# The second expert layer sorted by expert, with three of its four chunks routed inside the attention stage before it

## The chip, the cores and the metric

One core of a Trainium2 chip runs the whole program. The metric is device time in microseconds. TensorE (PE) multiplies, VectorE (DVE), ScalarE (ACT) and GpSimd (POOL) work on what it leaves, and SyncE (SP) issues most transfers. Each engine has its own queue and works it off in order; the queues meet at semaphores.

## The reference, cut to what matters

Input is 2048 tokens of 128 numbers. Six layers follow each other, each on the layer norm of the running sum `x`:

```python
x = x + 0.5 * expert_ffn(ln(x))      # first expert layer
x = x + attention_0(ln(x))           # 16 heads of 8, causal, then wo and bo
x = x + 0.5 * expert_ffn(ln(x))      # second expert layer: the one that is changed
x = x + 0.5 * ternary_ffn(ln(x))
x = x + attention_1(ln(x))
x = x + 0.5 * ternary_ffn(ln(x))

def expert_ffn(x):
    expert = argmax(softmax(x @ Wr.T))               # one of 8 per token
    inter = gelu(x @ W1[expert] + b1[expert])        # 128 -> 512, for each token its own expert
    y = inter @ Wo + bo + x
    return layer_norm(y) * gamma + beta
```

## The kernel before, in words

Tokens are cut into 16 blocks of 128 and 4 chunks of 512 (`NB`, `NCH`, `CH`, `BPC` = 4 blocks per chunk). Each layer is a function that writes one piece of program for every engine. `order` is the order in which a layer takes the chunks; a layer may make some of the next layer's norms (`Norms.make`, `given` says how many are there when the layer begins).

*Expert layer* (`expert_layer`, L282). For each chunk TensorE transposes the normed rows (L399) and makes the router's logits (L408). VectorE chooses an expert per token (`choose`, L651 to L667) as a one-hot row. Then all 8 experts are run over all 512 tokens: TensorE spreads an expert's 0/1 mask over the partitions (L428), ScalarE copies it (L587), VectorE masks both halves of the split input (L839), and TensorE adds three 512-column matmuls for each of the 4 tiles of the hidden layer (L443). A token of another expert gives zeros, so the sum over experts is the right expert's. Biases (L453), gelu (L578), down projection (`down`, L467), and `finish` on VectorE (L676 to L686): sum, norm, gamma, add to `x_res`. The input is split into a high and a low float16 part so that float16 matmuls keep the accuracy.

*Attention stage* (`attention_layer`). Work is written out in turns. A turn has one "quad" (128 keys against up to 512 queries of one group of four heads): scores (L1237 and L1186 are its matmuls with the running maxima), exps on ScalarE (L1319), values (L1215). Beside it stand some "units": scores of a later step whose row maxima VectorE takes (`part_max`, L1356). A step is a group of heads and a chunk of queries; `STEPS` lists them, and `units_beside_quads` deals the units out over the turns so that each step's maxima are there in time. When a step has ended, its output is scaled (L1385, L1389); after a chunk's last step come "turned" and "project", with the sum into `x_res` (L1360 to L1365). Three PSUM banks are used in rotation for all of this (the ring), and TensorE waits for VectorE to have read a bank.

*Ternary layer* (`ternary_layer`). Transposes (L890), ScalarE's high part (L933), VectorE's low part (L964), up matmuls (L914), relu (L942), down (L899), sum into `x_res` (L982). Norms that are not given are made between the low parts.

## Time and profile before

| | us |
|---|---|
| median of 3 runs | 1215.2 (1214.64 to 1215.71) |
| the profiled execution | 1215.68 |
| its span | 1213.9 |
| TensorE busy | 1091.9 (90%) |
| VectorE busy | 1006.6 (83%) |
| ScalarE busy | 664.6 (55%) |
| GpSimd busy | 65.8 (5%) |
| mean granted TensorE clock | 0.975 |

The span is from the first to the last instruction; 1.8 us of the execution lie around it. Busy time is a sum over stages with different limits, so the table is read stage by stage. The granted clock is 1.0 at 2.4 GHz and 0.5 at 1.2 GHz.

### The profile page before, as it was taken

Reading aid. Unit: us, or ns where it says so; the run is one execution under the profiler, and the core shown is the slowest. Engines: PE = TensorE matmul, PEld = TensorE weight load, DVE = VectorE, ACT = ScalarE, POOL = GpSimd, SP = SyncE. Lnnn points to the kernel's source line nnn. Section 1 sums busy time; section 2 is a strip of 40 time slices with the busy share of each in tenths; the row PEclk is TensorE's granted clock in tenths of the full one; section 3 lists DMA queues with packets and bytes.
Section 4 is the critical chain, followed back from the end, with each engine's and each line's share of the span. In section 5 each row is a group of like instructions: output and inputs, shape, how many; then the busy total and the mean of one; then the engine's idle time right before and its main releaser. Section 6 shows DMA issues by size and latency. Waiting matters only on the chain.

```text
span 1213.9 us, 34232 instructions
## 1 busy us (share of the span) xinstructions
PE 1091.9 (90%) x14757; PEld 492.3 (41%) x14757; DVE 1006.6 (83%) x2343; ACT 664.6 (55%) x861; POOL 65.8 (5%) x62
## 2 busy tenths in 40 slices
PE   1898976999999999999699987689999999999988
PEld 1455552333333333334345555433333333333436
DVE  8977568999999999886547657799999999998764
ACT  0322222556777777777332214145667777887773
POOL 5111001000000000000100100100000000000000
PEclk9999988999999999999799998899999999999999
DMA  5100034100000000000000000620000000000001
GB/s 158 36 1 1 1 98 117 33 3 2 2 3 2 3 2 3 3 2 3 1 1 2 1 1 1 181 64 3 2 3 2 2 2 2 3 2 3 4 3 35
DMA packets 23555, 24.07 MB, mean 20 GB/s; under 512 B 3134, under 2 KB 21220, under 8 KB 23404
## 3 DMA queue, kind: packets, MB, share of 16 engines
q1 hardware_dynamic: 22252, 18.73, 5.4%
q0 software_dynamic: 1152, 3.15, 1.0%
q8 instruction: 116, 1.90, 0.7%
q14 instruction: 35, 0.29, 0.1%
HBM read 13.20 MB, written 8.39 MB: 18 GB/s over the span
## 4 chain that ended last, share of the span: by engine, by line
PE 55%; DVE 37%; issue 4%; ACT 3%; DMA 1%; SPq 0%; DVEq 0%; ACTq 0%
DVE part_max L1356 25%; PE psum L1215 12%; PE psum L1237 11%; PE psum L443 10%; PE psum L1186 6%; PE psum L467 3%; ACT hidden L1319 2%; PE psum L1201 2%; PE psum L899 2%; PE psum L1243 1%; DVE xn L168 1%; PE psum L1264 1%; DVE norm_v L151 1%; PE psum L914 1%; PE psum L428 1%
## 5 line engine op out<-in xcount | busy, mean ns | idle before, releaser
L1356 DVE TENSOR_REDUCE part_max<-psum 128x1 f32<-128x512 f32 (+3 forms) x1120 | 677.1, 668 | 52.7 <-PE psum L1243 35.3
L1319 ACT ACTIVATE hidden<-psum 128x1024 f32<-128x1024 f32 (+3 forms) x640 | 539.0, 895 | 220.8 <-PE psum L1186 219.7
L1237 PE MATMUL psum<-k_slots,q_slots 128*32 128x512 f16 (+3 forms) x5120 | 389.9, 355 | 31.4 <-DVE part_max L1356 13.5
L1215 PE MATMUL psum<-hidden,v_aug 128*9 128x512 f32 (+3 forms) x2560 | 290.3, 530 | 0.1
L1237 PEld LDWEIGHTS psum<-k_slots,q_slots 128*32 128x32 f16 x5120 | 123.3, 95 | 286.2 <-DVE part_max L1356 193.1
L443 PE MATMUL psum<-parts,w_parts 128*128 128x512 f16 x768 | 179.5, 385 | 1.9 <-DVE parts L839 1.9
L1186 PE MATMUL psum<-q_slots,k_slots 32*128 32x512 f16 (+3 forms) x1472 | 141.3, 328 | 9.6 <-ACT hidden L1319 7.7
L443 PEld LDWEIGHTS psum<-parts,w_parts 128*128 128x128 f16 x768 | 73.6, 99 | 82.4 <-issue 5.7
L587 ACT CAST parts<-psum 128x512 f16<-128x512 f32 x64 | 37.2, 588 | 107.1 <-PE psum L428 107.1
L1243 PE MATMUL psum<-ident_bf,later_keys 128*32 128x128 bf16 (+2 forms) x1408 | 91.5, 250 | 0.0
L1186 PEld LDWEIGHTS psum<-q_slots,k_slots 32*128 32x128 f16 x1472 | 42.0, 91 | 99.7 <-ACT hidden L1319 49.0
L1201 PE MATMUL psum<-later_keys,ident_bf 128*32 128x128 bf16 x2048 | 74.8, 223 | 4.4 <-ACT hidden L1319 1.9
L1215 PEld LDWEIGHTS psum<-hidden,v_aug 128*9 128x9 f32 x2560 | 61.6, 90 | 34.9 <-ACT hidden L1319 1.6
L839 DVE TENSOR_TENSOR parts<-parts 128x1024 f16<-128x1024 f16 x64 | 46.8, 755 | 18.3 <-ACT parts L587 18.2
L1201 PEld LDWEIGHTS psum<-later_keys,ident_bf 128*32 128x32 bf16 x2048 | 39.7, 95 | 50.5 <-issue 19.4
L1243 PEld LDWEIGHTS psum<-ident_bf,later_keys 128*32 128x32 bf16 x1408 | 38.4, 99 | 18.6 <-issue 17.5
L625 POOL TENSOR_TENSOR x_plus<-xn,bo_bc 128x512 f32<-128x512 f32 x8 | 13.8, 1722 | 517.2 <-DVE xn L168 478.5
L245 ACT COPY xn_t<-psum 128x512 f32<-128x512 f32 x8 | 4.7, 588 | 57.0 <-PE psum L220 57.0
L467 PE MATMUL psum<-wo_sb,hidden 128*128 128x128 f32 x256 | 31.7, 285 | 3.7 <-ACT hidden L578 3.7
L954 POOL TENSOR_TENSOR x_plus<-x_res,fb_half 128x512 f32<-128x512 f32 x8 | 10.0, 1265 | 447.0 <-DVE xn L168 447.0
L467 PEld LDWEIGHTS psum<-wo_sb,hidden 128*128 128x128 f32 x256 | 31.3, 201 | 5.6 <-ACT hidden L578 4.7
L676 DVE TENSOR_TENSOR x_plus<-psum,x_plus 128x512 f32<-128x512 f32 x8 | 5.5, 691 | 33.8 <-PE psum L467 33.8
(168 smaller groups left out, 731.4 us busy)
## 6 DMA issues: line engine op xcount, KB each, us to landing
q_slots<-q_rows SPq DMA_DIRECT2D x8, 512.0 KB, 3.8
k_slots<-k_rows POOLq DMA_DIRECT2D x24, 128.0 KB, 4.2
q_rows<-parts SPq DMA_DIRECT2D x18, 128.0 KB, 3.0
k_rows<-parts SPq DMA_DIRECT2D x18, 128.0 KB, 2.8
q_slots<-in_L_ffn_W_dram SPq DMA_DIRECT2D x2, 1024.0 KB, 6.5
k_slots<-k_rows SPq DMA_DIRECT2D x8, 128.0 KB, 4.0
q_slots<-nm_parts SPq DMA_DIRECT2D x64, 4.0 KB
out_dram<-x_res SPq DMA_DIRECT2D x4, 256.0 KB, 2.3
```

Source lines behind the costliest of these rows:

```text
L443: last = pe.matmul(psum[:, t, :], w1_parts[:, e, wp, t * P:(t + 1) * P], x_mask[:, k % NX, xp, :], start=(e == 0 and (wp, xp) == (0, 0)), ...
L467: last = pe.matmul(psum[:, DOWN_BANK, i * D:(i + 1) * D], hidden[:, n % 2, t, i * P:(i + 1) * P], wo2_sb[:, t, :], start=(t == 0), stop=(t ...
L587: act.copy(mask_sb[:, k % NX, :], psum[:, MASK_BANKS + k % 2, :]).then_inc(mask_ready, 1)
L839: dve.tensor_tensor(x_mask[:, k % NX, :, :], x_parts[:, n % 2, :, :], mask_sb[:, k % NX, :].rearrange("p (a t) -> p a t", a=1).broadcast_t ...
L899: last = pe.matmul(psum[:, 6 + n % 2, i * D:(i + 1) * D], hidden[:, n % 2, t, i * P:(i + 1) * P], tw2_t[:, t, :], start=(t == 0), stop=(t ...
L1186: last = pe.matmul(psum[:, S_BANKS + 2 * (tile % 2) + par, cols], k_slots[rows, G * g + 2 * pr + par, j * P:(j + 1) * P], q_slots[rows, g, ...
L1201: last = pe.matmul(psum[rows32(m), S_BANKS + 2 * (tile % 2) + par, off:off + P], ident_bf[:, rows32(m)], later_keys[:, :], start=(pr == 0) ...
L1215: last = pe.matmul(psum[VW * h:VW * h + DH + 1, O_BANK, off:CH], v_aug[:, j, G * g + h, :], probs[:, (2 * n + h // 2) % NP, h % 2, off:CH] ...
L1237: last = pe.matmul(psum[rows32(m), bank, a * w:(a + 1) * w], q_slots[:, g, qb * P + m * SLOT:qb * P + (m + 1) * SLOT], k_slots[:, G * g + ...
L1243: last = pe.matmul(diagonal_part(psum[rows32(m), bank, 0:heads * w], heads), later_keys[:, rows32(m)], repeated(ident_bf, heads), start=Fa ...
L1319: act.activation(probs[:, tile % NP, :, off:CH], psum[:, bank:bank + 2, off:CH], ACT.Exp, scale=scale).then_inc(exp_done, 1)
L1356: dve.tensor_reduce(part_max[:, step_no[s] % 2, h0:h0 + heads, i, kc], psum[:, bank, 0:heads * w].rearrange("p (a k) -> p a k", a=heads), ...
```

## The change

The second expert layer is now `sorted_expert_layer`. It sends each token's normed row to a place that depends on its expert, and runs one expert over tiles of 128 tokens that all belong to it.

1. *Routing* (`Router`). Per chunk: transposes, logits, choice, and "ranks": small matmuls with a triangular matrix count how many earlier tokens chose the same expert. The result is a row number in `expert_regions`, a DRAM tensor with room for 2048 rows per expert, that is zeroed at the start of the program. GpSimd scatters the rows with an indirect DMA per block (L1202). Three chunks (3, 0, 2) are routed in late turns of the first attention stage; the fourth (chunk 1) is normed and routed in the expert layer.
2. *Table* (`tile_table`). From the counts: which expert and which rows each of 24 tiles has. 24 is enough whatever the choices are.
3. *Tiles.* SyncE reads a row number into a register per tile and loads 128 rows (L1317). Six groups of four tiles go through TensorE. The expert's weights are picked by a register on TensorE (L1110, L1122). Input parts are split two groups ahead, in three buffers.
4. *Way back.* Norm on VectorE, gamma on GpSimd, a store in sorted order (L1321), and then 16 indirect DMAs fetch each token's row (L1217). The next layer's norm adds it to `x_res` first.
5. *Orders.* The second half of the attention steps takes chunks 3, 0, 2, 1 in place of 3, 2, 1, 0, in both attention stages. Both give three norms to the next layer in place of two, each cut into six pieces over six turns. The ternary layer behind the experts is given one norm in place of three.

```diff
@@ Norms.make
+                if self.arrived:
+                    rows = slice(chunk * BPC, (chunk + 1) * BPC)
+                    dve.wait_ge(self.arrived[chunk], 16 * BPC)
+                    own.wait()
+                    own(dve.tensor_tensor(x_res[:, rows, :], x_plus[:, rows, :], x_res[:, rows, :], ALU.add))
@@ start of the program, SyncE
+                    zeros = k_slots[:, 2:2 + H // 2, :].rearrange("p h t -> p (h t)").bitcast(F32)
+                    for half in range(2):
...
@@ sorted_expert_layer, TensorE
+                def experts(n):
...
+                    chosen = [pe.value_load(tile_i[0:1, 0, n * BPC + i:n * BPC + i + 1], min_val=0, max_val=E - 1)
+                              for i in range(BPC)]
+                    pe.wait_ge(lo_ready, n + 1)
+                    for t in range(HT):
+                        if n >= 1:
+                            pe.wait_ge(gelu_done, HT * (n - 1) + t + 1)
+                        pe.matmul(psum[:, t, :], b1_parts[:, t * P:(t + 1) * P],
...
+                        for i in range(BPC):
+                            for wp, xp in ((0, 0), (0, 1), (1, 0)):
+                                weights = w1_parts[:, bass.ds(chosen[i], 1), wp, t * P:(t + 1) * P]
...
+                tile_table()
+                sorted_transposes(0)
+                sorted_transposes(1)
+                for n in range(TGROUPS):
+                    experts(n)
+                    if n + 2 < TGROUPS:
+                        sorted_transposes(n + 2)
+                    if n >= 1:
+                        down(n - 1)
+                down(TGROUPS - 1)
@@ GpSimd
+                    pool.wait_ge(router.placed, n + 1)
+                    for i in range(BPC):
+                        b = n * BPC + i
+                        pool.indirect_dma_start(out=region_dram, out_offset=bass.IndirectOffsetOnAxis(place[:, b:b + 1], 0),
+                                                in_=xn[:, lo + i, :], in_offset=None).then_inc(scattered, 16)
...
+                for c in next_norms.order:
+                    for i in range(BPC):
+                        b = order.index(c) * BPC + i
+                        pool.indirect_dma_start(out=x_plus[:, c * BPC + i, :], out_offset=None, in_=sorted_dram,
...
@@ SyncE
+                for k in range(TILES):
+                    start = sp.value_load(tile_i[0:1, 1, k:k + 1], min_val=0, max_val=E * T - P)
+                    if k == 0:
+                        sp.wait_ge(scattered, 16 * NB)
+                    sp.dma_start(x_sorted[:, k, :], region_dram[bass.ds(start, P), :]).then_inc(group_moved[k // BPC], 16)
@@ attention_layer
+        LAST_CHUNKS = (3, 0, 2, 1)
...
-                            norm_turn[idle + 1 + 3 * (NCH - 1 - c)] = c
+                            summed = turn + 2 if projected else turn
+                            for piece in range(Norms.PIECES):
+                                norm_turn[summed + 1 + piece] = c, piece
+            if router:
+                for turn, kind, n in ((152, "features", 0), (153, "logits", 0), (155, "ranks", 0),
+                                      (154, "features", 1), (156, "logits", 1), (158, "ranks", 1),
+                                      (158, "features", 2), (159, "logits", 2), (161, "ranks", 2)):
+                    tail.setdefault(turn, []).append((kind, n))
```

TensorE's queue where the second expert layer begins, before. L399 are transposes of a chunk's normed rows, L408 the logits, L428 masks, L443 the matmuls of one expert.

```order
L1258 MATMUL psum<-wo_sb,parts 128x128 x4
L391 UNCONDITIONAL_BRANCH
L399 MATMUL psum<-ident,xn 128x128 x4
L408 MATMUL psum<-wr_t,xn_t 128x8 x4
L417 MATMUL psum<-ident_bf,onehot 24x128 x4
L428 MATMUL psum<-ident_bf,onehot 128x128 x16
L443 MATMUL psum<-parts,w_parts 128x512 x12
```

The same queue now, behind the ranks of the last chunk. L1082 to L1092 are the table, L1102 the transposes of groups 0 and 1, L1110 and L1122 (TENSOR_LOAD, ISA) register loads and address work.

```order
L1082 MATMUL psum<-ones_bf,before 8x1
L1084 MATMUL psum<-tiles_bf,earlier 8x1
L1087 MATMUL psum<-tile_choice,expert_no 1x24
L1088 MATMUL psum<-tile_choice,tile_shift 1x24
L1089 MATMUL psum<-tile_choice,expert_rows 24x24
L1092 MATMUL psum<-shift_diag,ones_mat 128x8
L1102 MATMUL psum<-ident,q_slots 128x128 x8
L1110 TENSOR_LOAD tile_i
L1110 ISA x2
```

The pattern of one hidden tile in a group, now:

```order
L1116 MATMUL psum<-tile_experts,b_parts 128x512
L1122 ISA
L1122 MATMUL psum<-parts,w_parts 128x128 x2
L1122 ISA
L1122 MATMUL psum<-parts,w_parts 128x128
```

The 12 matmuls of 512 columns for one expert and one chunk have become 12 of 128 columns for four tiles, with an address instruction ahead of two and of one in turn. Both groups of transposes stand ahead of the first expert matmul.

GpSimd's queue from the last attention turns to the end of the layer, before (two sums for a chunk, then the ternary layer's):

```order
L1094 DMA k_slots<-k_rows 32x4x512 x12
L599 UNCONDITIONAL_BRANCH
L625 TENSOR_TENSOR x_plus<-xn,bo_bc 128x512
L627 TENSOR_TENSOR x_res<-x_res,beta_half 128x512
...
L949 UNCONDITIONAL_BRANCH
L954 TENSOR_TENSOR x_plus<-x_res,fb_half 128x512 x4
```

and now (L1202 the scatters, L1185 the sum with bo, L1191 gamma, L1217 the fetching of the rows):

```order
L1197 TENSOR_TENSOR x_res<-x_res,beta_half 128x512
L1202 DMA expert_regions<-xn,place 16384x128 x4
L1185 TENSOR_TENSOR x_plus<-q_slots,bo_bc 128x512 x2
L1191 TENSOR_TENSOR xn<-xn,gamma_half 128x512
...
L1185 TENSOR_TENSOR x_plus<-q_slots,bo_bc 128x512
L1191 TENSOR_TENSOR xn<-xn,gamma_half 128x512 x2
L1217 DMA x_plus<-sorted_rows,back 128x128 x16
L1401 UNCONDITIONAL_BRANCH
L1406 TENSOR_TENSOR x_plus<-x_res,fb_half 128x512 x4
```

GpSimd had two sums per chunk; it has twelve sums for six groups, and sixteen indirect DMAs on each side of them.

## Rows read from the trace of the kernel before

**Rows 1.** The page, the chain that ended last, by engine.

```profile
PE 55%; DVE 37%; issue 4%; ACT 3%; DMA 1%; SPq 0%; DVEq 0%; ACTq 0%
```

**Rows 2.** Windows of two stages: us, busy (count) per engine, granted clock, DMA share, GB/s.

```profile
203.00:599.00 396.00, 374.56 (x6214) 144.16 (x6206) 359.42 (x673) 275.76 (x336) 7.18 (x8) 0.99 0.03 7
599.00:733.00 134.00, 121.41 (x725) 69.12 (x726) 77.47 (x300) 35.75 (x62) 9.29 (x6) 0.95 0.00 1
```

**Rows 3.** Groups by line, 604 to 722 us: busy us, mean ns | idle before.

```profile
L443 PE MATMUL psum<-parts,w_parts 128*128 128x512 f16 x384 | 89.4, 384 | 0.0
```

**Rows 4.** Timeline at the attention stage's end: start us, us, engine, what.

```profile
576.63 0.87 DVE L142 BATCH_NORM_STATS2 norm_stats<-x_res 128x6 f32<-128x128 f32 x4
...
580.33 1.11 DVE L168 TENSOR_SCALAR xn<-x_res,norm_mean_var,norm_rstd 128x128 f32<-128x128 f32 x4
...
598.39 0.69 DVE L1365 TENSOR_TENSOR x_res<-psum,x_res 128x512 f32<-128x512 f32 x1
...
599.14 1.11 PE L399 MATMUL psum<-ident,xn 128*128 128x128 f32 x4 [1.51 <-DVE x_res L1365]
...
601.41 1.88 PE L408 MATMUL psum<-wr_t,xn_t 128*128 128x8 f32 x8 [1.16 <-ACT xn_t L564]
...
604.66 0.18 DVE L667 TENSOR_TENSOR onehot<-tied,top 128x32 bf16<-128x32 f32 x1
```

**Rows 5.** Timeline of VectorE in the ternary layer.

```profile
732.14 0.68 DVE L964 SCALAR_TENSOR_TENSOR parts<-psum,parts 128x512 f16<-128x512 f32 x1
...
744.79 0.69 DVE L982 SCALAR_TENSOR_TENSOR x_res<-psum,x_plus 128x512 f32<-128x512 f32 x1 [1.77 <-PE psum L899]
...
762.40 1.40 DVE L261 SCALAR_TENSOR_TENSOR hidden<-psum,bias_cols,hidden 128x512 f16<-128x512 f32 x2
```

**Rows 6.** GpSimd's transfers L1094: time from issue to landing.

```profile
L1094 POOL DMA_DIRECT2D k_slots<-k_rows x24: 550/550/690, 179.9 to 807.6; - x24
...
DMA to landing us min/median/max: 3.9/4.2/5.8
```

**Rows 7.** Transfers by line: KB each, median us to landing.

```profile
out_dram<-x_res SPq DMA_DIRECT2D x4, 256.0 KB, 2.3
```

**Rows 8.** Timeline of SyncE's queue.

```profile
14.05 0.43 SPq L375 DMA_DIRECT2D w_qkv<-in_L_attn_wv_dram  x1
```

**Rows 9.** Line L1306, ScalarE's register loads, ns min/median/max.

```profile
L1306 ACTq TENSOR_LOAD <-exp_scale x2: 295/386/477, 158.0 to 758.7; - x2
```

**Rows 10.** Chain that ended last, in the second expert layer: start, us, what.

```profile
637.42 0.44 PE psum L399 x4
...
641.70 2.59 PE psum L443 x12
...
673.92 3.57 PE psum L467 x32
```

**Rows 11.** Timeline of a mask's four matmuls.

```profile
695.76 0.39 PE L428 MATMUL psum<-ident_bf,onehot 128*128 128x128 bf16 x4
```

**Rows 12.** Line L428, duration of one, ns min/median/max.

```profile
L428 PE MATMUL psum<-ident_bf,onehot x256: 216/219/314, 30.5 to 707.9; 128*128 128x128 bf16 x128
```

**Rows 13.** Waits of the weight load queue: us, times, longest.

```profile
PEld psum L443 <- issue: 2.2, 8, 0.3
```

**Rows 14.** Timeline of ScalarE, ends of both attention stages.

```profile
584.35 1.94 ACT L1319 ACTIVATE hidden<-psum 128x1024 f32<-128x1024 f32 x2 [4.57 <-PE psum L1186]
...
590.08 1.08 ACT L1319 ACTIVATE hidden<-psum 128x512 f32<-128x512 f32 x2 [1.90 <-PE psum L1186]
...
1173.14 1.94 ACT L1319 ACTIVATE hidden<-psum 128x1024 f32<-128x1024 f32 x2 [0.47 <-PE psum L1186]
...
1177.67 2.03 ACT L1319 ACTIVATE hidden<-psum 128x512 f32<-128x512 f32 x4 [0.70 <-PE psum L1186]
```

**Rows 15.** Timeline of the first microseconds.

```profile
2.29 13.75 POOL L616 MEMSET k_slots<- 128x16384 int32 x1
...
4.95 11.10 DVE L151 TENSOR_SCALAR norm_v<-norm_mean_var 128x4 f32<-128x4 f32 x1
```

More of the change, by code:

```diff
@@ L156, in norm_rstd, with rstd_refine @@
             own.wait()
-            for _ in range(3):
+        def rstd_refine(dve, own, s, b0, n, times):
+            v, r, t = s.v[:, b0:b0 + n], s.rstd[:, b0:b0 + n], s.tmp[:, b0:b0 + n]
+            for _ in range(times):
                 own(dve.scalar_tensor_tensor(out=t, in0=r, scalar=-0.5, in1=r, op0=ALU.mult, op1=ALU.mult))
@@ L164, in norm_rstd @@
                 own.wait()
+        def norm_rstd(dve, own, s, eps, b0, n):
+            rstd_seed(dve, own, s, eps, b0, n)
+            rstd_refine(dve, own, s, b0, n, 3)
         def norm_apply(dve, s, dst, src, b):
@@ L179, in __init__ @@
                 self.ready, self.order = sem(name), order
+                self.arrived = None
             def wait(self, engine, chunk):
@@ L1068, in macaron_layers, with attention_layer @@
         TURNS += [(None, [])] * 5
-        def attention_layer(proj, layer, projected, given, next_norms, next_given, released):
+        def attention_layer(proj, layer, projected, given, next_norms, next_given, released, router=None):
             s1 = NormScratch("norm")
@@ L1131, in attention_layer @@
             PLAN = late_work()
-            idle = max(turn for turn, (_, turn_max, _, _) in enumerate(PLAN) if turn_max)
             tail, norm_turn = {}, {}
@@ L1249, in ring_item @@
                         last = pe.transpose(psum[0:G * BPC, bank, 0:P], neg_max[:, k % 2, :], ident[:, :])
+                    elif kind == "features":
+                        last = router.transposes(pe, psum[:, bank, :], what)
+                    elif kind == "logits":
+                        pe.wait_ge(ring_read, ring_no["features", what] + 1)
+                        last = router.logits(pe, psum[:, bank, :], what)
+                    elif kind == "ranks":
+                        last = router.ranks(pe, psum[:, bank, :], what)
                     elif kind == "turned":
```

438 lines of the change are left out of this document (398 added, 40 removed).

## The prediction

> **What bounds the kernel now.** I read the chain of waits on the page first: TensorE carries 55% of it, VectorE 37% [rows 1]. That is an average, so I cut the span into stages [rows 2]. The reader is to see that the first attention stage (396 us; TensorE 374.6 busy, VectorE 359.4; the second attention looks alike) holds both engines, and that the second expert layer (134 us) is TensorE's alone: 121.4 us busy there, VectorE 77.5. Then the groups by line inside that layer: 384 expert matmuls of 512 columns, 89.4 us of TensorE [rows 3]. Every expert is run over every token, and seven of eight results are masked to zero. Last I read the timeline at the layer's two ends. The last sum of the attention stage ends at 598.39 + 0.69 = 599.08 us, which I call T0 [rows 4]; the next attention layer's first low parts start at 762.40, with the ternary layer's first low part at 732.14 [rows 5]. So T0 to 762.40 is 163.3 us, and this is what the change rebuilds.
>
> **The sum, step by step from T0.** The new path is one long chain before and behind a shorter stretch of TensorE work.
>
> *Routing the last chunk.* Norm of chunk 1: 576.63 to 580.33 + 1.11, so 4.8 us [rows 4]. Transposes, copy, logits and choice took 599.14 to 604.84, 5.7 us [rows 4]; the new code has one ScalarE copy less ahead of the logits and one one-hot write instead of three, about 0.9 less: 4.8. The ranks are 18 small matmuls, which the trace doesn't show; the 8 of the logits took 1.88 [rows 4], and one at the pace of the 128-column slots below would be 0.057, so 1.0 to 4.2; I take 2.1. Four small VectorE operations at 0.19 [rows 4] with handoffs: 0.9. Places are known at T0 + 12.8 with 0.2 of waits.
>
> *Scatter.* Four indirect DMAs on GpSimd. None is in the trace. The nearest row is GpSimd's direct DMA, 0.55 us to issue and 3.9 to 5.8 to landing [rows 6]; SyncE's stores of the result land in 2.3 [rows 7]. An indirect one also reads 128 row numbers: 0.55 to 2.5 each, and I take 1.1. Landing 2.3 to 4.2, I take 3.3. So 4 x 1.1 + 3.3 = 7.7: T0 + 20.5. VectorE's and TensorE's table of tiles (13 small operations, some 5 us) lies beside it. The Trainium skill's page "DMA: Bandwidth & Descriptors", section "Anatomy of one DMA — SWDGE (gpsimd) path", gives about 2.0 us of fixed cost plus bytes over 436 GB/s, 2.15 us for one 64 KB transfer; by it the four hops of this path would be 3 us less in all than what I put, and by GpSimd's row of 4.2 they are 1.8 more. The trace's row is above the rule for the same queue.
>
> *Loading sorted tiles.* TensorE's queue has the transposes of groups 0 and 1 ahead of the first expert matmul, so eight tiles must land. SyncE issues one of 64 KB in 0.43 [rows 8], and loads a register for each (ScalarE's register load: 0.295 to 0.477 [rows 9]) with address work: 1.0 per tile, from 0.5 to 1.5. 0.45 + 7 x 1.0 + 2.4 landing = 9.9, and 0.6 for the second transposes: T0 + 31.0 (rounded). Later groups arrive every 4 us, faster than they are used.
>
> *Six groups on TensorE.* A group is 4 bias matmuls of 512 columns (2.59/12 = 0.216 each [rows 10]) and 48 of 128 columns. The mask matmuls show such a slot: 4 in 0.39 us, one by itself 0.219 [rows 11, 12], so (0.39 - 0.219)/3 = 0.057. Array time 4 x 0.216 + 48 x 0.057 = 3.6. But each group also has 32 address instructions and 4 register loads on TensorE's own queue, because the weights are picked by a register. The trace has none of them there. The low end is 0 (hidden in the queue). The high end is the gap that TensorE's queue shows after a wait instruction, 2.2 us in 8 times, 0.28 each [rows 13]: 32 x 0.28 + 4 x 0.48 = 10.9. I take one 128-column slot, 0.057, for each address instruction (1.8) and hide the loads behind the down projection: 5.4 per group. Down is 3.57 and transposes 0.44 [rows 10]. 6 x (5.4 + 3.57) + 4 x 0.44 = 55.6, and 2 us for matmuls at half clock after the idle stretch (the windows grant 0.95 over the old layer [rows 2]). T0 + 88.6. VectorE needs 0.7 + 0.7 + 4.8 = 6.2 per group, below TensorE's 9.4, with GpSimd's two sums beside it.
>
> *The way back.* VectorE is one group behind: group 5's norm ends 2 x 5.6 - 3.57 = 7.7 after the last matmul. Scale on GpSimd 1.3, store 2.8, then four gathers like the scatters 7.7: 19.5, T0 + 108.1. Sum and norm of chunk 0, 5.5; cold transposes 1.1, high part 0.6, low part 0.7, waits 0.2: 8.1. The ternary layer's first low part ends at T0 + 116.2; before it ended at T0 + 133.7.
>
> *The ternary layer.* Three chunks instead of one are summed and normed inside it. Each is 5.5 us, and a low part waits behind it (transposes and ScalarE copy 1.7, low part 0.7): 2 x 7.9 + 5.5 = 21.3, and 1.4 for GpSimd's last sum. From the first x_res sum on it is 744.79 to 762.40, 17.6 [rows 5], as before. 40.3 in place of 29.6. The rebuilt stretch ends at T0 + 156.5: 163.3 - 156.5 = 6.8 us gained.
>
> *The attention stages.* Before, whole norms stand in the way of the last turns: ScalarE waited 4.57 and 1.90 us at two exps of the first attention, where the second shows 0.47 and 0.70 [rows 14]. The pieces take this away: -5.3. Twelve steps of routing come in: VectorE 3 x 3.4 us, in turns that have no maxima. I charge a third, +3.4, from 0 to 10.2, and -0.6 for one unit less beside late quads. Net -2.5. In the second attention only the order changes: 0, from -2 to +2. The last ternary layer is TensorE's from its second chunk on, and that chunk waits for the same norm as before: 0.
>
> *The start.* Eleven small GpSimd operations behind the k_slots memset. VectorE's L151 took 11.10 us beside that memset of 13.75 [rows 15]: it ended when the memset did. One more such wait on a 0.4 us memset: +0.4. The zeros (8.4 MB to DRAM) are the only new work on SyncE's queue there, and what waits for them, the first scatter, comes hundreds of us later: 0.
>
> Sum: -6.8 - 2.5 + 0.4 = -8.9 on the profiled execution's 1215.68, so 1206.8. The median of the runs shown is 0.5 lower; I say **1207**.
>
> **Rivals.**
> 1. *Array pace.* TensorE's address instructions hide altogether. Group 7.6 us instead of 9.4: 6 x 1.8 = 11 more, 1196. For: the queue runs ahead during the down projection. Against: in the expert stretch they come two for three matmuls. The skill's page "SBUF — State Buffer", section "SBUF: two separate sides", calls the port pair of VectorE and GpSimd an exclusive lock held for a whole instruction; [rows 15] agrees. By it the two GpSimd sums of a group (1.3 each) could add 2.6 to VectorE's 6.2, make that the pace (8.8) and leave 1203 of this rival, while my forecast stays.
> 2. *Addressing is the bound (slower).* Register-addressed weight loads and their address instructions set TensorE's pace. It decides from 5.4 + 8.9/6 = 6.9 us per expert group on; at 9 us it is 6 x 3.6 = 22 more, 1229. For: 8 address instructions to 12 weight loads in one in-order queue, with an issue gap of 0.28 in the trace [rows 13]. Against: the fixed-address pairs of this kernel issue every 0.057 [rows 11].
> 3. *The DMA chain.* Indirect DMAs at 2.5 us: 8 on the path, 8 x 1.4 = 11 more, 1218.
> 4. *It doesn't shorten.* If tiles arrive slower than used (over 2.3 us per tile on SyncE), groups follow SyncE: at 3 us, 6 x 2.8 = 17 more, 1224. Little speaks for it.
>
> **Chances.** Forecast 0.48, rival 1 0.23, rival 2 0.14, rival 3 0.10, rival 4 0.05. Of the forecast 0.04 and of rival 3 0.02 fall within 0.2% (2.4 us), which is about what a measurement can tell from no change. Faster by more 0.67, same 0.06, slower 0.27. Range: rival 1 with short landings (-7) at the low end, 1189; rival 2 at the high end, 1229. The forecast's own range is 1200 to 1214.
>
> **What would show it.** Expert matmuls of a group 5.4 us from first to last; first expert matmul 31 us behind the attention's last sum; a gap of 25 to 30 us on TensorE between the last down projection and the first ternary matmul; the 4.57 us wait gone; granted clock at half in both gaps. I am wrong if an expert group takes over 7 us, or if the two gaps together are over 75 us.

## The result and the profile after

| | before | after |
|---|---|---|
| median, us | 1215.15 (1214.64 to 1215.71, 4 runs) | 1223.2 (1222.43 to 1224.05, 4 runs) |
| ratio | | 1.0059 [1.0047, 1.0071] |
| span of the profiled execution | 1213.9 | 1221.1 |
| mean granted clock | 0.975 | 0.952 |

The kernel is 0.6% slower; the forecast was 1207. Of all the executions behind this document one, of e16, fell far out (1960.85 us), and it is left out of e16's median and ratio. The windows of the two stages, in the columns of [rows 2]:

```profile
203.00:599.00 396.00, 379.19 (x6276) 146.83 (x6268) 365.28 (x728) 275.45 (x335) 15.77 (x17) 1.00 0.03 9
599.00:733.00 134.00, 71.86 (x620) 57.24 (x616) 61.51 (x280) 27.98 (x43) 39.84 (x38) 0.74 0.13 36
```

The second window holds the rebuilt stretch, which changed as it was meant to: TensorE 71.9 us busy where it had 121.4, and the clock at 0.74 for it. But the attention's window is fuller than before on TensorE (379.2 against 374.6), VectorE (365.3 against 359.4) and GpSimd (15.8 against 7.2).

VectorE's timeline (start, us, engine, line; idle before in brackets) has the stretch's marks. The rows answer to [rows 4] and [rows 5]:

```profile
605.28 0.69 DVE L1844 TENSOR_TENSOR x_res<-psum,x_res 128x512 f32<-128x512 f32 x1
...
719.16 0.69 DVE L1416 SCALAR_TENSOR_TENSOR parts<-psum,parts 128x512 f16<-128x512 f32 x1 [1.90 <-ACT parts L1385]
...
724.34 2.85 DVE L190 TENSOR_SCALAR xn<-x_res,norm_mean_var,norm_rstd 128x128 f32<-128x128 f32 x4
...
744.13 0.69 DVE L1434 SCALAR_TENSOR_TENSOR x_res<-psum,x_plus 128x512 f32<-128x512 f32 x1 [1.43 <-issue]
...
763.40 1.40 DVE L400 SCALAR_TENSOR_TENSOR hidden<-psum,bias_cols,hidden 128x512 f16<-128x512 f32 x2
```

T0 is now 605.28 + 0.69 = 605.97, against 599.08. The next attention's low parts start at 763.40, against 762.40. So the rebuilt stretch takes 157.43 us in place of 163.32.

TensorE inside it (the transposes of group 1, the first expert matmul, a group of the steady state, the last down projection, the first ternary transposes), then SyncE's loads and GpSimd's first and last scatter of chunk 1 and its first and fourth gather:

```profile
633.79 1.12 PE L1102 MATMUL psum<-ident,q_slots 128*128 128x128 f32 x4 [3.17 <-DMA q_slots<-expert_regions]
636.59 0.60 PE L1116 MATMUL psum<-tile_experts,b_parts 128*128 128x512 bf16 x1 [1.68 <-DVE parts L1267]
...
663.01 0.38 PE L1116 MATMUL psum<-tile_experts,b_parts 128*128 128x512 bf16 x1 [0.80 <-issue]
...
667.43 0.63 PE L1102 MATMUL psum<-ident,q_slots 128*128 128x128 f32 x4
667.89 3.74 PE L1134 MATMUL psum<-wo_sb,hidden 128*128 128x128 f32 x32
672.52 0.38 PE L1116 MATMUL psum<-tile_experts,b_parts 128*128 128x512 bf16 x1 [0.89 <-issue]
...
690.62 3.81 PE L1134 MATMUL psum<-wo_sb,hidden 128*128 128x128 f32 x32 [0.88 <-DVE x_plus L1276]
717.40 1.09 PE L1342 MATMUL psum<-ident,xn 128*128 128x128 f32 x4 [22.97 <-DVE xn L190]
```

```profile
624.18 15.84 SPq L1317 DMA_DIRECT2D q_slots<-expert_regions  x15
```

```profile
617.96 0.98 POOL L1202 DMA_INDIRECT expert_regions<-xn,place  x1 [5.58 <-DVE place L322]
...
621.77 0.96 POOL L1202 DMA_INDIRECT expert_regions<-xn,place  x1 [0.30 <-issue]
...
705.25 1.01 POOL L1217 DMA_INDIRECT x_plus<-sorted_rows,back  x1 [3.13 <-DMA sorted_rows<-xn]
...
709.08 0.94 POOL L1217 DMA_INDIRECT x_plus<-sorted_rows,back  x1 [0.30 <-issue]
```

The first expert matmul is 30.6 us behind T0. The profile puts the 1.68 us ahead of it down to VectorE's low part of group 1, but the program waits there for group 0's alone, which had ended at 631.97; e8 shows below what the wait is. A group takes 672.52 - 663.01 = 9.51 us. TensorE is then empty from 694.4 to 717.4.

In the second attention, ScalarE's first and last exps and VectorE's last maximum, after, and then the two of them before that [rows 14] doesn't hold:

```profile
799.96 1.94 ACT L1788 ACTIVATE hidden<-psum 128x1024 f32<-128x1024 f32 x2 [1.08 <-PE psum L1648]
...
1184.79 2.03 ACT L1788 ACTIVATE hidden<-psum 128x512 f32<-128x512 f32 x4 [0.36 <-PE psum L1648]
```

```profile
1166.18 0.69 DVE L1825 TENSOR_REDUCE part_max<-psum 128x1 f32<-128x512 f32 x1
```

```profile
799.00 1.94 ACT L1319 ACTIVATE hidden<-psum 128x1024 f32<-128x1024 f32 x2 [1.08 <-PE psum L1186]
```

```profile
1165.25 0.69 DVE L1356 TENSOR_REDUCE part_max<-psum 128x1 f32<-128x512 f32 x1 [0.73 <-PE psum L1243]
```

From the first exp to the last one the stage took 1177.67 + 2.03 - 799.00 = 380.70 us and takes 386.86. The maxima end at the same distance from its start (366.94 and 366.91); what follows them takes 13.76 before and 19.95 now.

All of it together, in us of span:

| piece | forecast | measured |
|---|---|---|
| start, to the first exp (203.53, 203.54) | +0.4 | 0.0 |
| first attention, first exp to T0 | -2.5 | +6.9 |
| T0 to the next attention's low parts | -6.8 | -5.9 |
| second attention, first to last exp | 0 | +6.2 |
| last ternary layer | 0 | +0.1 |
| sum | -8.9 | +7.2 |

### The profile page after: what moved, and what is told of

Read it like the earlier page. It is cut to its first block and busy times, and to the rows that moved or that the text cites. A ratio compares the mean times of both kernels' runs of the same rounds, so it can differ in the third digit from the quotient of the medians.

```text
span 1221.1 us, 34564 instructions
## 1 busy us (share of the span) xinstructions
PE 1045.2 (86%) x14691; PEld 480.8 (39%) x14691; DVE 995.4 (82%) x2390; ACT 652.1 (53%) x832; POOL 106.6 (9%) x114
## 5 line engine op out<-in xcount | busy, mean ns | idle before, releaser
L1699 PE MATMUL psum<-k_slots,q_slots 128*32 128x512 f16 (+3 forms) x5120 | 390.4, 354 | 37.8 <-DVE part_max L1825 18.8
L587 PE MATMUL psum<-parts,w_parts 128*128 128x512 f16 x384 | 89.7, 384 | 1.9 <-DVE parts L1000 1.9
L587 PEld LDWEIGHTS psum<-parts,w_parts 128*128 128x128 f16 x384 | 36.8, 99 | 42.2 <-issue 2.8
L731 ACT CAST parts<-psum 128x512 f16<-128x512 f32 x32 | 18.6, 588 | 55.1 <-PE psum L572 55.1
L1406 POOL TENSOR_TENSOR x_plus<-x_res,fb_half 128x512 f32<-128x512 f32 x8 | 10.1, 1268 | 395.6 <-DVE xn L190 395.6
L1394 ACT ACTIVATE hidden<-psum,bias_cols 128x512 f32<-128x512 f32 x32 | 20.6, 687 | 24.7 <-PE psum L1366 24.5
L1173 ACT ACTIVATE hidden<-psum,unscale 128x512 f32<-128x512 f32 x24 | 16.5, 687 | 31.4 <-PE psum L1122 31.4
L1342 PE MATMUL psum<-ident,xn 128*128 128x128 f32 x32 | 6.0, 318 | 30.9 <-DVE xn L190 30.1
L1197 POOL TENSOR_TENSOR x_res<-x_res,beta_half 128x512 f32<-128x512 f32 x4 | 5.1, 1272 | 310.4 <-DVE xn L190 310.3
L1351 PE MATMUL psum<-tw_t,hidden 128*128 128x128 f32 x256 | 30.1, 277 | 0.0
```

What stands on the lines that cost most here:

```text
L587: last = pe.matmul(psum[:, t, :], w1_parts[:, e, wp, t * P:(t + 1) * P], x_mask[:, k % NX, xp, :], start=(e == 0 and (wp, xp) == (0, 0)), ...
L731: act.copy(mask_sb[:, k % NX, :], psum[:, MASK_BANKS + k % 2, :]).then_inc(mask_ready, 1)
L1173: act.activation(hidden[:, n % 2, t, :], psum[:, t, :], ACT.Gelu, scale=unscale[:, 0:1]).then_inc(gelu_done, 1)
L1351: last = pe.matmul(psum[:, 6 + n % 2, i * D:(i + 1) * D], hidden[:, n % 2, t, i * P:(i + 1) * P], tw2_t[:, t, :], start=(t == 0), stop=(t ...
L1394: act.activation(hidden[:, n % 2, t, :], psum[:, t, :], ACT.Relu, bias=fb1_col[:, t:t + 1], scale=1.0 / X_SCALE).then_inc(relu_done, 1)
L1699: last = pe.matmul(psum[rows32(m), bank, a * w:(a + 1) * w], q_slots[:, g, qb * P + m * SLOT:qb * P + (m + 1) * SLOT], k_slots[:, G * g + ...
```

## The experiments

Sixteen of the eighteen kernels start from the changed one; e4 starts from the one before, and e13 is the changed kernel itself. The table gives each one's profile by stage, cut at the same marks. A1 is the first attention from its first exp to T0, split into the time to VectorE's last maximum, from there to the last exp ("end"), and on to T0. E is T0 to the next attention's low parts. A2 is the second attention to its last maximum, and its end.

| | median | ratio to before | A1 | E | A2 |
|---|---|---|---|---|---|
| before | 1215.2 | | 369.0 + 19.7 + 6.9 | 163.3 | 366.9 + 13.8 |
| changed | 1223.2 | 1.0059 [1.0047, 1.0071] | 370.3 + 25.3 + 6.9 | 157.4 | 366.9 + 20.0 |
| e1 | 1225.6 | 1.0071 [1.0051, 1.0092] | 370.3 + 31.1 + 8.9 | 157.5 | 368.6 + 13.8 |
| e2 | 1223.6 | 1.0064 [1.0041, 1.0086] | 373.2 + 23.0 + 6.7 | 160.8 | 368.8 + 13.8 |
| e3 | 1231.9 | 1.0129 [1.0107, 1.0150] | 370.3 + 31.1 + 8.9 | 157.0 | 361.4 + 27.2 |
| e4 | 1219.5 | 1.0019 [1.0006, 1.0033] | 369.1 + 18.4 + 7.8 | 163.5 | 361.8 + 20.7 |
| e5 | 1218.0 | 1.0024 [1.0014, 1.0033] | 370.3 + 25.4 + 7.2 | 156.9 | 361.8 + 19.5 |
| e6 | 1220.9 | 1.0039 [1.0023, 1.0055] | 370.3 + 25.4 + 7.3 | 157.1 | 367.2 + 13.8 |
| e7 | 1229.6 | 1.0115 [1.0096, 1.0133] | 370.3 + 19.1 + 8.7 | 169.0 | 367.0 + 18.8 |
| e8 | 1211.0 | 0.9957 [0.9940, 0.9973] | 371.4 + 25.4 + 7.2 | 143.9 | 366.9 + 18.8 |
| e9 | 1229.8 | 1.0120 [1.0099, 1.0142] | 368.4 + 32.9 + 8.7 | 158.1 | 367.0 + 20.2 |
| e10 | 1226.5 | 1.0085 [1.0068, 1.0102] | 371.5 + 31.3 + 8.9 | 153.4 | 366.9 + 18.8 |
| e11 | 1229.9 | 1.0121 [1.0104, 1.0137] | 370.2 + 31.3 + 8.9 | 156.7 | 366.9 + 18.8 |
| e12 | 1222.1 | 1.0052 [1.0032, 1.0073] | 368.4 + 32.7 + 9.8 | 153.6 | 367.1 + 13.8 |
| e13 | 1229.4 | 1.0105 [1.0088, 1.0122] | 370.3 + 31.2 + 8.9 | 157.4 | 367.0 + 18.8 |
| e14 | 1233.3 | 1.0139 [1.0122, 1.0156] | 370.3 + 31.3 + 8.9 | 159.7 | 367.0 + 20.0 |
| e15 | 1222.3 | 1.0042 [1.0028, 1.0057] | 371.5 + 31.3 + 8.9 | 153.4 | 367.0 + 13.8 |
| e16 | 1225.9 | 1.0076 [1.0056, 1.0096] | 370.3 + 31.4 + 8.9 | 156.2 | 367.0 + 13.8 |
| e17 | 1230.4 | 1.0123 [1.0105, 1.0141] | 371.4 + 29.6 + 8.7 | 158.1 | 367.0 + 20.0 |
| e18 | 1222.5 | 1.0054 [1.0033, 1.0075] | 370.3 + 29.5 + 8.9 | 155.3 | 367.0 + 13.8 |

One thing must be read first. e1 to e4 and e9 to e12 ran on one chip, e5 to e8 on a second, e13 to e18 on a third. On the second, the first attention's end has the 25.4 us of the first measurement, and some 7 to T0: the short form. On the other two the same code takes 31.2, and 8.9 to T0: the long form. After its first measurement the changed kernel itself was run again only on the third, as e13. So totals are compared within a chip, and stages across chips only where that end isn't in them. Each profile is one execution, and the same code differs in it by about 1 us a stage: the second attention, left as changed, ends in 18.8 to 20.2 us, and the first one's maxima take 370.3 or 371.4.

### The second attention: e1 to e6

e1: `orders = (UP, UP, (3, 0, 2, 1), TURNING, TURNING, (3, 2, 1, 0))`, and the steps made from each layer's own order.

> The changed kernel with the second half of the second attention's steps back in the order 3, 2, 1, 0 (and the last ternary layer in that order); all else as changed. Theory A (the order: when VectorE's last maxima are taken, 11 quads are left in place of 8, because the last step has eight quads and not four; that stretch was 13.8 us before and is 19.9 now): the second attention gives back its 6.2 us, 1223.2 - 6.2 = 1217.0. Theory B (the norms cut into pieces, or one norm more inside the stage, slow the turns): the order doesn't matter, within 1 us of 1223.2. The first attention stays 6.9 us longer under both.

e2: both orders (3, 2, 1, 0), and the third chunk's routing at turns 166, 167 and 168.

> Both attention stages back in the order 3, 2, 1, 0; the chunks 3, 2 and 1 are routed (the third one only in the turns behind the last quads, since its sum comes late), chunk 0 in the expert layer. Theory A: 6.2 us less in the second attention and 4.7 in the first (its stretch behind the last maximum was 26.3 us and is 31.1), against which the third chunk's routing now stands at the stage's end, some 2 us of VectorE: 1223.2 - 10.9 + 2 = 1214, from 1212 to 1216. Theory B: 1223 or above, since the routing then stands on the path.

The total is 1223.6, not 1214. The second attention takes 382.5, as in e1. The first has the order of the kernel before and still takes 402.9 us to T0, 7.4 more than there: its maxima end 4.2 later and its end is 3.4 longer. So the order isn't what lengthens it. E is 3.3 longer than in e1, with the third chunk's routing behind the last quads. e1 and e3 take 410.3 to T0 on the same chip with the changed order, so the long form isn't the chip's alone.

e3: the last of the orders is (3, 1, 0, 2).

> The changed kernel with the second attention's last steps in the order 3, 1, 0, 2, so that the last step has 12 quads. Theory A: 15 quads are left behind the last maxima, four full ones more at about 2 us: 1223.2 + 8 = 1231. Theory B: as many norms and pieces as before, within 1 us of 1223.2.

Its total, 1231.9, is theory A's 1231 by luck: the second attention takes 388.6 us, only 1.7 more than in the changed kernel, and the rest is the first attention's long form, 7.9 more.

e4, in the kernel before:

```diff
-orders = (UP, UP, BETWEEN, TURNING, TURNING, DOWN)
+orders = (UP, UP, BETWEEN, TURNING, TURNING, (3, 0, 2, 1))
-norm_turn[idle + 1 + 3 * (NCH - 1 - c)] = c
+norm_turn[idle + 1 + 3 * next_norms.order.index(c)] = c
```

> The kernel before, with nothing changed but the order 3, 0, 2, 1 in the second attention (two norms given, each whole, as before). Theory A: 1215.2 + 6.2 = 1221.4. Theory B: no pieces and no further norm, so 1215.2.

The ends came as theory A has them: 13.8 us where the last step has four quads, 20.7 with eight, 27.2 with twelve. But theory A's sums failed. In e4 the stage took 1.8 us more, not 6.2, since VectorE's last maximum comes 5.1 us sooner when the last step is a longer one. The rows of e4, ScalarE's and VectorE's:

```profile
798.53 1.94 ACT L1324 ACTIVATE hidden<-psum 128x1024 f32<-128x1024 f32 x2 [1.08 <-PE psum L1191]
...
1178.97 2.03 ACT L1324 ACTIVATE hidden<-psum 128x512 f32<-128x512 f32 x4 [0.37 <-PE psum L1191]
```

```profile
1159.62 0.69 DVE L1361 TENSOR_REDUCE part_max<-psum 128x1 f32<-128x512 f32 x1 [0.25 <-PE psum L1248]
```

The last maximum ends 361.78 behind the first exp, where the changed kernel has 366.91 with the same order. Something in the changed kernel takes these 5.1 us back, and it isn't the order. e1 fits: with the order back the stage takes 382.35, still 1.65 above before. That left the norms, laid beside the maxima in pieces:

```diff
@@ e5: second attention alone
-norm_turn[summed + 1 + piece] = c, piece
+late = max(turn + 1, idle + 1 + 3 * next_norms.order.index(c)) + piece // 2
+norm_turn.setdefault(late, []).append((c, piece))
```

> The changed kernel, order 3, 0, 2, 1 kept, with the three norms that the second attention gives to the last layer moved behind its last maxima (three turns each, two pieces in a turn). Theory C (two causes in the second attention: the order alone costs 1.8 us, as the kernel before with that order showed, 382.47 against 380.70; norm pieces laid beside the maxima keep VectorE from them, 366.9 us in place of 361.8 to the last one): the last maximum comes at 361.8 us behind the first exp, the stage takes 382.5, the kernel 1223.2 - 4.3 = 1218.9. Theory A (order alone): no change.

> As the last one, and the second attention's order back to 3, 2, 1, 0. Theory C: the stage takes 380.7 us as in the kernel before, so that the kernel takes 1223.2 - 6.2 = 1217.0. Theory A: the same as with that order alone, where the stage took 382.35 us. The first attention is unchanged, but may take 5.8 us more where a second stretch at the half clock falls into its end.

e5's rows:

```profile
798.63 1.94 ACT L1793 ACTIVATE hidden<-psum 128x1024 f32<-128x1024 f32 x2 [1.08 <-PE psum L1653]
...
1177.88 2.03 ACT L1793 ACTIVATE hidden<-psum 128x512 f32<-128x512 f32 x4 [0.36 <-PE psum L1653]
```

```profile
1159.76 0.69 DVE L1830 TENSOR_REDUCE part_max<-psum 128x1 f32<-128x512 f32 x1 [0.25 <-PE psum L1710]
```

361.82 to the last maximum and 381.28 in all: theory C. e7 and e8, on e5's chip, have the second attention as changed and take 385.7, so laying the norms late gives back 4.4 there. The 6.2 us have two causes, the order and the pieces of norms laid where VectorE has no time to give, but they don't simply add. With the norms late the order costs 0.3 (e5 against e6) to 1.8 (e4 against before). The pieces cost 1.4 with the order 3, 2, 1, 0 (e1's 382.4 against e6's 381.0) and 4.4 to 5.6 with 3, 0, 2, 1. Why they cost more with the second order wasn't taken apart. e5's total is 5.2 below the changed kernel's 1223.2, against 4.3 expected, though that one was measured at another time. In e6 the stage takes 381.0 as expected; its total misses, since from the last exp on it takes 38.4 us for 34.3, with the third norm now made behind the last quads.

### The first attention: e7, e9, e13, e17

e7: `(164, "features", 0), (165, "logits", 0), (167, "ranks", 0)` and so on to `(170, "ranks", 2)`, with four more empty turns.

> The changed kernel with all nine routing items of the first attention moved behind its last quad (turns 164 to 170). Theory D (routing is what lengthens the end of that stage: its small matmuls and ScalarE-free turns make TensorE and ScalarE wait for VectorE): from the first exp to the last one 370.3 + 25.3 = 395.6 us falls to about 387 (the second attention with the same order: 386.9), no stretch at the half clock before the last exp; the norms' cost stays. The routing then stands on the path, 3 x 4 us or so more between the last exp and the first expert matmul. Rival: it is the projection and norms of this stage, and the stage's end stays within 1 us of 395.6.

VectorE's last maximum and ScalarE's last exps of e7, then the two of the changed kernel:

```profile
571.33 0.69 DVE L1825 TENSOR_REDUCE part_max<-psum 128x1 f32<-128x512 f32 x1
```

```profile
589.08 2.03 ACT L1788 ACTIVATE hidden<-psum 128x512 f32<-128x512 f32 x4 [0.36 <-PE psum L1648]
```

```profile
573.10 0.69 DVE L1825 TENSOR_REDUCE part_max<-psum 128x1 f32<-128x512 f32 x1
```

```profile
597.07 2.03 ACT L1788 ACTIVATE hidden<-psum 128x512 f32<-128x512 f32 x4 [1.02 <-PE psum L1648]
```

The end is 591.11 - 572.02 = 19.1 in place of 25.3: 6.2 us are the routing's. Theory D holds in that, but for another reason than it gave. That end as a window, in the kernel before, in the changed one and in e7 (columns as in [rows 2]):

```profile
572.55:592.21 19.66, 15.08 (x247) 6.75 (x243) 12.92 (x59) 11.16 (x18) 4.46 (x4) 0.91 0.01 3
```

```profile
573.79:599.10 25.31, 23.48 (x344) 10.71 (x342) 13.47 (x65) 17.01 (x24) 12.35 (x12) 0.93 0.07 25
```

```profile
572.02:591.11 19.09, 16.68 (x252) 5.64 (x249) 5.63 (x30) 16.99 (x24) 0.00 (x0) 1.00 0.01 2
```

ScalarE has the same exps in the changed kernel and in e7, 17.0 us; TensorE has 6.8 more in the changed one, and the end is 6.2 longer. The rows also show what became of the forecast's gain. The kernel before has 11.2 us of exps in this end and stalls between them. e7 has hardly a stall, but 5.8 us more of exps, because the last step has eight quads: with the 4.57 us wait gone, its end is only 0.6 shorter. The changed kernel's TensorE timeline:

```profile
588.54 0.66 PE L260 MATMUL psum<-ident,xn 128*128 128x128 f32 x4
...
590.15 1.03 PE L266 MATMUL psum<-wr_t,xn_t 128*128 128x8 f32 x8 [0.62 <-DVE xn_t L1829]
...
595.12 0.18 PE L277 MATMUL psum<-region_rows,ones_bf 128*128 128x8 bf16 x1
...
595.65 0.62 PE L1677 MATMUL psum<-hidden,v_aug 128*9 128x512 f32 x4
```

Transposes 0.66, logits 1.03, ranks 595.65 - 595.12 = 0.53: 2.2 us of TensorE for a chunk, 6.7 for three, in a stretch where TensorE has no time to spare (23.5 us busy of 25.3). That fits the 6.2 us; what VectorE's and GpSimd's parts of the routing, which e7 moves too, add to it isn't separated. In e7 the routing stands behind the last exp and costs 1.8 more up to T0 and 11.5 behind it.

e9: `late = 151 + 3 * next_norms.order.index(c) + piece // 2` for the first attention, and the routing from turn 155 on.

> The changed kernel with the first attention's three norms laid behind its last maxima (turns 151 to 159, two pieces a turn) and its routing three turns later for that. Theory C (norm pieces beside maxima hold VectorE up, in this stage as in the second, where moving them gave 5.1 us): the last maximum 370.3 - 4.5 = 365.8 us behind the first exp; the stage's end 25.4 as now, since its routing costs TensorE's own time (6.3 us) wherever it stands in it; so 1223.2 - 4.5 = 1218.7. Rival: the norms now hold up the routing and the last turns, and what the maxima gain is lost behind them, 1223.

The rival is right. The last maximum gained 1.9 us and the end took 1.6 back (32.9 against 31.3 in e10 and e11). What is a gain in a stage that has an idle VectorE at its end is none where that end is full of routing.

e13 has no edit.

> The changed kernel itself, on the chip of the next three. If the first attention's end takes its second stretch at the half clock here (31.3 us behind the last maximum and 8.9 to the projection's sum, in place of 25.3 and 6.9), it takes 1223.2 + 8 = 1231; if not, 1223.

It took the long form, on another chip. ScalarE's timeline of e13 at the last quads, and the windows of both kernels at the same place (columns as in [rows 2]):

```profile
592.82 1.02 ACT L1788 ACTIVATE hidden<-psum 128x1024 f32<-128x1024 f32 x1 [2.38 <-PE psum L1663]
594.31 2.50 ACT L1788 ACTIVATE hidden<-psum 128x1024 f32<-128x1024 f32 x3 [0.47 <-remote]
...
603.31 0.66 ACT L1788 ACTIVATE hidden<-psum 128x256 f32<-128x256 f32 x2 [2.35 <-remote]
```

```profile
596.00:600.00 4.00, 4.00 (x56) 1.52 (x58) 0.73 (x5) 1.41 (x3) 1.94 (x2) 0.57 0.05 16
```

```profile
596.00:600.00 4.00, 3.47 (x74) 1.24 (x66) 0.52 (x4) 2.28 (x6) 2.62 (x3) 1.00 0.10 33
```

Exps start 0.47 and 2.35 us late with no TensorE row that explains it ("remote"), and then the granted clock falls to half while quads are still to do, where the changed kernel of the first measurement kept 1.00. In both forms GpSimd's twelve scatters run from about 582 on, so in e13 the first odd wait comes some 9 us behind the first scatter. e17 holds them back: `pool.wait_ge(router.placed, max(n + 1, NCH - 1))`.

> The changed kernel with GpSimd's first scatter waiting for the third chunk's places (596.4 us in the changed kernel's profile) in place of the first chunk's (582.7). Its twelve scatters at 1.27 us end some 5 us before the last chunk's places come, so that nothing later waits for them. If their traffic is what holds up the first attention's last quads in the long form, the end takes 25.3 us or less in every run, 1223 or below. Rival (the half clock and its place in time alone): 31.2 us and 1229 are seen again as in e13.

```profile
592.64 3.42 ACT L1788 ACTIVATE hidden<-psum 128x1024 f32<-128x1024 f32 x4 [1.12 <-PE psum L1648]
597.41 0.60 ACT L1788 ACTIVATE hidden<-psum 128x512 f32<-128x512 f32 x1 [1.35 <-PE psum L1663]
...
602.59 0.66 ACT L1788 ACTIVATE hidden<-psum 128x256 f32<-128x256 f32 x2 [3.09 <-remote]
```

```profile
596.00:603.25 7.25, 3.26 (x66) 1.11 (x58) 0.54 (x4) 1.91 (x5) 5.35 (x6) 1.00 0.11 36
```

The first scatter is now issued at 596.8. Up to the exps at 592.64 the steps are those of the short form to within 0.15 us; the odd waits begin behind that scatter (3.09 us "remote" at 602.59). So here the odd waits begin with GpSimd's indirect DMAs. They are as large as soon as these run: the end is 29.6 us and the time no better, nearer to the rival than to the expectation. But the rival's cause, the half clock, is out in this profile, since the granted clock is 1.00 from 596 to 603.25, where the waits are. That the scatters are the cause isn't shown: e13 had them for 9 us without an odd wait, and the short form has the same twelve with none. What makes two chips stall and one not stays open.

### The expert layer: e8, e10, e11, e14

e8: `chosen = [(n + i) % E for i in range(BPC)]`, `w1_parts[:, chosen[i]:chosen[i] + 1, ...]`. It leaves out the reading of each tile's expert, so it doesn't compute the layer's result.

> The changed kernel with the expert of each tile fixed in the program (weights of expert (group + tile) mod 8) in place of read into a register, so that the experts applied are not those of the tokens; as many matmuls. Forecast of the addressing's cost: 1.8 us per group (5.4 against 3.6): 6 x 1.8 = 11 us less, 1212. Rival array pace: none of it shows, the four tiles of a group take 4.5 us as now, and only the gap of 0.55 to 0.9 us ahead of each group goes: 6 x 0.8 = 5 us less, 1218.

```profile
635.17 1.12 PE L1102 MATMUL psum<-ident,q_slots 128*128 128x128 f32 x4 [3.24 <-DMA q_slots<-expert_regions]
636.08 0.63 PE L1115 MATMUL psum<-tile_experts,b_parts 128*128 128x512 bf16 x1
...
649.15 0.38 PE L1115 MATMUL psum<-tile_experts,b_parts 128*128 128x512 bf16 x1
...
652.69 0.61 PE L1102 MATMUL psum<-ident,q_slots 128*128 128x128 f32 x4
...
656.71 0.38 PE L1115 MATMUL psum<-tile_experts,b_parts 128*128 128x512 bf16 x1
```

Four hidden tiles take 3.54 us in place of 4.42 (663.01 to 667.43), and the wait of 0.80 to 0.89 ahead of a group, put down to "issue", is gone: 7.56 a group against 9.51. That is 1.95 per group, where the forecast had 1.8, so the price of picking weights by a register was right in sum. Its parts weren't: address work costs 0.88 and not 1.8, and the four register loads are not hidden but stand ahead of the group. Ahead of group 0 they cost more: from the start of group 1's transposes to the first expert matmul it is 0.91 us here and 2.80 in the changed kernel, so 1.9 are the loads', and the 1.68 us wait there is theirs and not VectorE's. The whole stretch is 13.0 us shorter than e5's on the same chip, 143.9 against 156.9; 11 were expected.

e10: `sorted_transposes(1)` behind `t == 1` of `experts(0)`, ScalarE's `high_part(1)` behind its second gelu.

> The changed kernel with the transposes of tile group 1 (and its high part) behind the second hidden tile of group 0, in place of ahead of its first matmul. The rows show group 1's tiles landing 4.3 us behind group 0's and the first expert matmul waiting for them: 636.59. It should come 4.3 us sooner, at 31.0 - 4.3 = 26.7 us behind the attention's last sum, and the last down projection about 3.5 us sooner; 1219.7. Rival: TensorE is at the half clock there and the group takes as much longer.

The first expert matmul comes 4.3 us sooner behind T0 and E takes 153.4: 4.0 less than in e13 (another chip, E alone). The first group runs mostly at the half clock as before (a mean granted clock of 0.71 from 641 to 650, 0.68 at the same place in the changed kernel), and little is given back. The total, 1226.5 for 1219.7 expected, has the long form in it.

e11: GpSimd's first `x_plus` sum of the ternary layer ahead of the last four gathers.

> The changed kernel with GpSimd's sum x_plus of the ternary layer's first chunk ahead of its last four gathers in place of behind them. If the 2.85 us of VectorE's normed rows at 724.34 (1.11 elsewhere) come from GpSimd's sum starting beside them at 725.06, that duration is 1.11 and the ternary layer 1.7 us shorter: 1221.5. Rival: it is the gathers' own traffic, and it stays at 2.85.

VectorE's normed rows took 1.11 us again, but its sum x_res at 725.40 then took 2.15 in place of 0.68, beside GpSimd's sum at 725.71. The collision moved; E is 0.7 shorter than in e13. The 1.11 alone would prove little, since e13's has it too (1.12 at 722.73): there GpSimd's sum starts at 731.67, and a VectorE operation of 0.16 us takes 0.90 beside it. In each of these profiles the long VectorE operation is the one beside that sum.

e14: `fill(16)`, `fill(20)`, `fill(84)`, each `psum[:, 3, :]` from `w1_parts`, 128x512.

> The changed kernel with matmuls of 512 columns that nobody reads in the expert layer's waits on TensorE: 16 ahead of the last chunk's transposes, 20 behind the table of tiles, 84 behind the last down projection. If the half clock costs there what its rows show (a hidden tile of group 0 takes 1.70 us and one of the others 1.05; transposes 1.11 and 0.66; the ternary layer's first up matmuls 3.59 and 1.89), the first group gains 2 us, and the ternary layer's first two chunks 0.5 each of their transposes: about 3 less than e13. Rival: nothing, since VectorE's norms set the pace there, or a loss, where the filling runs past what it waits for.

The first expert matmul came 1.2 us sooner than in e13, but E grew by 2.3, to 159.7. VectorE's norm of the second chunk is what grew:

```profile
729.06 0.17 DVE L166 TENSOR_SCALAR norm_v<-norm_mean_var 128x4 f32<-128x4 f32 x1 [1.21 <-DVE norm_mean_var L160]
730.47 0.17 DVE L168 TENSOR_SCALAR norm_tmp<-norm_v 128x4 int32<-128x4 int32 x1 [1.23 <-DVE norm_v L166]
```

Operations of 0.17 us wait 1.2 us for the one before them on their own engine, while GpSimd issues gathers (to 731.1). So the loss that the rival names came, but not by its cause: the filling ended at 718.6, and TensorE then waited 4.88 us for VectorE's norm, so it ran past nothing. Nor did the clock hold: the ternary layer's first transposes took 1.09 us as before. Why VectorE waits there wasn't tested. In total e14 is 3.9 us slower than e13.

### Put together: e12, e15, e16, e18

e12 is e9, e10, e11 and the second attention as before; e15 is e10 and that second attention; e16 is e15 with e14; e18 is e15 with e17. None met its forecast.

> All together: e9, e10, e11, and the second attention as in the kernel before (order 3, 2, 1, 0, two norms given, whole, behind the last maxima). By the sum of the parts: -4.5 - 3.5 - 1.7 - 6.2 = -15.9 on 1223.2: 1207.3, which would be 0.65% below the kernel before.

> The changed kernel with the second attention as in the kernel before (order 3, 2, 1, 0, two norms, whole, behind the last maxima: 380.7 us) and the first expert matmul ahead of group 1's transposes (e10: 153.4 us in place of 157.4 to the next attention). 6.2 + 4.1 = 10.3 less than e13: 1213 where e13 shows 1223, 1221 where it shows 1231.

> e15 with the filled gaps of e14. About 3 us less than e15, by the rows at either clock; 1210 where e13 shows 1223.

> e15 (second attention as in the kernel before, first expert matmul ahead of group 1's transposes) with the scatters held as in e17. e15 took 1222.3 with the long end; with the short one 8 us less: 1214. Rival: 1222 again.

e15 is 7.1 us below e13 on the same chip, 10.3 expected. By the spans (1227.3 and 1221.3) the second attention gave 5.0 and E 4.0; the first attention took 1.2 more, the start and the last ternary layer 0.9 each. It is still 0.4% above the kernel before. e18 is no faster. e12 took 1222.1 where 1207.3 was expected: the long form is 8 us of that, and the gains of e9 (4.5) and e11 (1.7) didn't come, as in those runs. e16 is 3.7 slower than e15 in place of 3 faster, with VectorE's waits of e14 (1.2 us) again. Of all eighteen only e8, which isn't the layer, is below the kernel before: the price of the register-picked weights is larger than what is missing.

## Why the prediction was wrong

The range (1189 to 1229) held 1223.2; the sign was wrong, and slower had 0.27. Point by point:

- *Routing, scatter, loads.* Right in sum, by two errors that cancel: the first expert matmul came 30.6 us behind T0, for 31.0. Group 1's tiles had landed at T0 + 27.8, where the forecast's terms give 30.4. But from there to the first expert matmul it was 2.8 us where 0.6 was put, 1.9 of it TensorE's register loads, which the forecast had hidden. The first scatter of chunk 1 was issued at T0 + 12.0 (12.8); a scatter takes 0.96 and 0.30 between two, 1.27 for 1.1; it lands in 2.2 where 3.3 was put. The Trainium skill's page "DMA: Bandwidth & Descriptors", section "Anatomy of one DMA — SWDGE (gpsimd) path", gives 2.15 for such a transfer: there the page was nearer than the row that I took. The 24 tile loads take 26.13 us on SyncE, 1.09 each, for 1.0.
- *Six groups.* Right: from the first expert matmul to the end of the last down projection 57.8 us, for 57.6. The parts cancel as e8 shows: 4.42 us from a group's first expert matmul to its last, where 5.4 was put, and 0.8 to 0.9 of register loads ahead of it, where nothing was.
- *Way back.* 25.4 us to the end of the first low part, for 27.6: the first gather is issued 1.0 sooner than the terms give, and the four gathers take 1.4 less, again the landing. TensorE's gap is 23.0 us, below the 25 to 30 that were named.
- *Ternary layer.* 719.85 to 763.40 is 43.6 us, for 40.3. 1.7 are VectorE's 2.85 us of normed rows at 724.34 beside GpSimd's sum; the rest lies behind the first `x_res` sum (744.13 to 763.40 is 19.3 us, 17.6 in [rows 5]) and wasn't taken apart.
- *The attention stages: the step that failed.* "The pieces take this away: -5.3 ... I charge a third, +3.4 ... Net -2.5. In the second attention only the order changes: 0". The wait of 4.57 us did go. But I priced the new order at the stalls it removed, and the second attention at its order alone, though the change puts pieces of a third norm and of the other two into both stages. Three things were left out. More quads stand behind the last maxima when the last step has eight of them: in the second attention 6.9 us there and 5.2 less before it, 1.8 in all by e4, and in the first 5.8 us of exps in place of the stalls (e7). Pieces of norms moved from VectorE's idle end into the time that its maxima fill are not free (some 5 us in the second attention, e5; in the first, moving them late gave 1.9 back to the maxima and nothing in all, e9). And routing is TensorE's work too, 2.2 us a chunk, in an end where TensorE is as full: 6.2 by e7, where the sum had 3.4 for VectorE. That gives 6.9 and 6.2 in place of -2.5 and 0: 15.6 of the 16.1 us by which the sum missed. Without the routing the first attention would still be 2.5 us longer than before (e7's 398.1 to T0 against 395.6), where the terms without it gave -5.9.
- *Small slips.* The change lays nine routing items in the first attention, not twelve. The forecast of 1206.8 less the 0.5 between profile and median is 1206 and not 1207. No run shows a dearer start: it is 0.0 for +0.4.
- *Rivals.* Array pace is out (group 9.5 us). Addressing stayed below the 6.9 us from which it decides: 5.3. The DMA chain and SyncE's pace are out. The range held 1223.2 only because rivals that didn't come true stretched it. The loss came from none of them, but from work that I had taken for hidden.

## What to carry to other kernels

Work dealt out beside a full engine is not free because it is cut into small pieces: ask, for each engine it touches and for each stretch it is moved from and to, whether that engine waits there, and charge it where it doesn't: here 6.2 of 6.7 us on TensorE, and some 5 us for two norms and part of a third, of 4.8 us each, on VectorE. When the order of steps changes, count what is left to do behind the last item of the engine that sets the pace, and what that item gains by coming sooner: in e4 6.9 us behind it and 5.2 ahead. And a gain in one stretch (here 5.9 us from running one expert per tile) is easily smaller than what the neighbours pay to prepare it.

## What the runs showed of the hardware

- A hidden tile (a bias matmul of 512 columns, 0.22 us, and 12 matmuls of 128 columns) takes 0.88 us with weights at fixed addresses (e8) and some 1.1 with weights picked by a register. By my estimate that is 0.055 and 0.07 us for each of the 12. Four register loads ahead of them leave the array idle for 0.8 to 0.9 us, and 1.9 ahead of the first group.
- An indirect DMA of 128 rows of 512 bytes costs GpSimd 0.96 us plus 0.30 to the next and lands in 2.2 (scatter) or 2.5 us (gather), medians of 16 each in the changed kernel.
- Beside them other engines started late in some profiles: ScalarE up to 3.09 us (e17), VectorE 1.2 us between dependent operations of 0.17 (e14). That the indirect DMAs are the cause isn't shown. The same first attention took 402.9 us on one chip (e5) and 410.5 on another (e13), while the kernel before, which has no indirect DMA, had medians of 1215.6 to 1217.4 on all three.
- A VectorE operation beside a GpSimd sum of 1.27 us grew from 1.11 to 2.85 us (changed kernel), and from 0.68 to 2.15 (e11).
